# Fixing eight expert tiles in advance instead of four, over two experts, in a fused attention and mixture-of-experts kernel

## What is computed

```python
x = x + ((1-g)*layernorm(x) + g*(A + A.T)/2)   # per batch; A = sigmoid(sim) where sim is among
                                                # the 153 largest of its row, else 0
h = layernorm(x)                                # now 2048 tokens
logits = h @ router_weight.T + router_bias      # 16 experts
top_val, top_idx = top_k(logits, 4); score = softmax(top_val)
for each token and each of its 4 experts e:
    gate, up = split(h @ gate_up_proj[e] + gate_up_bias[e])      # 512 -> 2 x 512, interleaved
    gate = min(gate, 7); up = clip(up, -7, 7)
    y = ((up + 1) * gate * sigmoid(1.702*gate)) @ down_proj[e] + down_bias[e]
    out[token] += score * y
out = x + out
```

## Time and profile before

| | us |
|---|---|
| runs of the kernel before | 915.58 median, 914.37 to 919.76, 3 runs |
| the profiled execution | 910.78 |
| its span in the trace | 909.0 |

### The profile page before, as it was taken

How to read it: one execution, slowest core, us unless ns; L and a number is a source line. 1 busy time by engine, 2 the same in 40 slices (tenths; PEclk the granted TensorE clock), 3 DMA queues, 4 the chain that set the end, 5 groups by cost and what they waited for, 6 DMA issues and landing times.

```text
span 909.0 us, 16747 instructions
## 1 busy us (share of the span) xinstructions
PE 768.3 (85%) x3566; PEld 622.4 (68%) x3567; DVE 595.4 (65%) x1068; ACT 403.4 (44%) x663; POOL 311.6 (34%) x352
## 2 busy tenths in 40 slices
PE   5354825256699999999999999999999999999993
PEld 2123524245588888878888887887788878888882
DVE  3678948397484855875757667577757565766542
ACT  2999758622142523353333524435533253442221
POOL 1331736475323322232323333332323222332221
PEclk9765655556799999999999999999999999999998
DMA  8501102115564552655736465586557445632332
GB/s 279 196 1 47 47 12 82 48 48 159 151 162 122 140 136 55 179 165 141 210 64 191 111 187 133 136 217 185 144 163 187 95 101 164 177 94 47 57 58 42
DMA packets 70706, 112.06 MB, mean 123 GB/s; under 512 B 29894, under 2 KB 32198, under 8 KB 70598
## 3 DMA queue, kind: packets, MB, share of 16 engines
q1 hardware_dynamic: 32454, 74.22, 23.5%
q0 software_dynamic: 18416, 36.53, 20.3%
q10 hardware_dynamic: 19728, 0.15, 1.2%
HBM read 84.05 MB, written 28.90 MB: 124 GB/s over the span
## 4 chain that ended last, share of the span: by engine, by line
PE 72%; ACT 11%; DVE 5%; another core or an unknown queue 4%; issue 4%; POOL 2%; ACTq 1%; DMA 1%; DVEq 0%; SPq 0%; POOLq 0%
PE gate_up_ps L852 40%; PE bank L852 22%; PE bank L842 3%; PE bank L834 3%; ACT marks L518 3%; ACT bgu L518 3%; PE bank L736 1%; ACT x_sb L531 1%; POOL step_u L412 1%; ACT w L655 1%; ACT A L528 1%; ACT xn L549 1%; DMA gam<-n_L_xattn_gamma_raw_dram 1%; PE gate_up_ps L741 0%
## 5 line engine op out<-in xcount | busy, mean ns | idle before, releaser
L852 PE MATMUL gate_up_ps<-w,xh 128*128 (+1 forms) x1152 | 364.5, 398 | 1.5 <-DVE xl L1032 1.5
L852 PEld LDWEIGHTS gate_up_ps<-w,xh 128*128 128x128 f32 x1152 | 212.6, 190 | 42.8 <-issue 1.9
L437 POOL DMA_INDIRECT out_dram<-yb,aslot x72 | 131.9, 1832 | 286.8 <-ACT yb L636 254.0
L852 PE MATMUL gate_up_ps<-w,xl 128*128 (+1 forms) x576 | 226.2, 393 | 0.0
L852 PE MATMUL bank<-w,hh 128*128 (+1 forms) x576 | 179.5, 393 | 7.3 <-DVE hl L1037 6.2
L629 ACT ACTIVATE sg<-gc 128x512 f32<-128x512 f32 x72 | 45.6, 634 | 228.5 <-DVE gc L1047 211.7
L1043 DVE TENSOR_TENSOR gu<-gate_up_ps,bgu 128x1024 f32<-128x1024 f32 x72 | 88.1, 1224 | 76.5 <-PE gate_up_ps L852 47.4
L428 POOL DMA_INDIRECT xg<-xn_rows,gslot x75 | 76.1, 1015 | 179.1 <-DMA gslot<-slot_rows 149.3
L852 PEld LDWEIGHTS bank<-w,hh 128*128 128x128 f32 x576 | 107.1, 188 | 35.8 <-issue 14.1
L1037 DVE TENSOR_TENSOR hl<-bank,hh 128x512 fp32r<-128x512 f32 x72 | 49.5, 688 | 117.3 <-ACT hh L623 105.6
L852 PEld LDWEIGHTS gate_up_ps<-w,xl 128*128 128x128 f32 x576 | 108.9, 189 | 23.6
(11 more groups left out here) (209 smaller groups left out, 796.0 us busy)
## 6 DMA issues: line engine op xcount, KB each, us to landing
raw_w<-_L_ffn_gate_up_proj_dram SPq DMA_DIRECT2D x64, 512.0 KB
raw_w<-in_L_ffn_down_proj_dram SPq DMA_DIRECT2D x64, 256.0 KB
bgu<-n_gate_up_proj_bias_dram SPq DMA_DIRECT2D x16, 512.0 KB
x_sb<-in_x_dram SPq DMA_DIRECT2D x4, 1024.0 KB, 11.5
xn_rows<-xn SPq DMA_DIRECT2D x4, 1024.0 KB
out_dram<-x_sb SPq DMA_DIRECT2D x4, 1024.0 KB
xg<-xn_rows,gslot POOLq DMA_INDIRECT x75
out_dram<-yb,aslot POOLq DMA_INDIRECT x72
```

The source lines that it names most:

```text
L437: pool.indirect_dma_start(out_v, bass.IndirectOffsetOnAxis(aslot[:, k, 0:1], 0), yb[:, k % 2, :], None, bounds_check=TOKENS - 1, oob_is_er ...
L852: last = nc.tensor.matmul(out_ps, lhs[:, rows], w[:, bass.ds(buf, 1), part, c, cols].rearrange("p a d -> p (a d)"), start=(m == 0), stop=( ...
```

## The change

Eight tiles are fixed in advance: tiles 0 to 3 are the first four of expert 0, tiles 4 to 7 the first four of expert 1, all filled from batches 0 to 2. Behind them come the other tiles of expert 0, those of expert 1 (one at least), then experts 2 to 15 as before. The table of words so has 18 segments for 16 experts, with two small rows of corrections (`steps`, `rooms`) for where a segment's slots begin. Experts 0 and 1 hold the two buffers of `w` through the first four segments, so no weights move for the two extra changes of expert. `gslot` of tiles 4 to 7 is loaded by SP from fixed addresses between and behind expert 1's raw halves, and `gslot` of tiles 8 to 10 by the table. POOL gathers tile 4 before it waits for the write of x. Steps 4 to 7 are written without reads of the table on every engine. `split_first` stays in steps 2 and 3.

```diff
-FROZEN = UNROLL
+FROZEN = 2 * UNROLL
+SEGS = E + FROZEN // UNROLL
...
+        def first_block(T):
+            return T // UNROLL * (TOKENS // P) + T % UNROLL
...
             if known(T, FROZEN) and row == 0:
-                return 0
+                e, e_before = T // UNROLL, max(T - 1, 0) // UNROLL
+                return e | e << FIELDS["bias"][0] | e_before % 2 << FIELDS["buffer_before"][0]
...
                         sp.wait_ge(S["lo_done"], HALF * (h + 1))
                         load_half(1, h, 1)
+                        for T in range(UNROLL + 2 * h, UNROLL + 2 * h + 2):
+                            sp.wait_ge(gathered[T % UNROLL], 16)
+                            sp.dma_start(gslot[:, T % UNROLL, :], slot_d[first_block(T) * P:(first_block(T) + 1) * P, :]
+                                         ).then_inc(gslot_in[T % UNROLL], 16)
...
-            for T in range(1, UNROLL):
+            for T in range(FROZEN - 3, FROZEN):
                 k = (T + 3) % UNROLL
-                sp.wait_ge(gathered[k], 16)
+                sp.wait_ge(gathered[k], 32)
...
-            for T in range(FROZEN):
+            for T in range(UNROLL):
                 gather(T, T)
             scatter(NB, NT * TOP_K)
+            gather(UNROLL, 0)
+            pool.wait_ge(S["acc_out"], 16 * NB)
+            add(0, 0)
             pool.wait_ge(S["xn2_out"], 16 * NB)
-            pool.wait_ge(S["acc_out"], 16 * NB)
-            for T in range(1, FROZEN):
+            for T in range(2, FROZEN):
                 gather(T + 3, (T + 3) % UNROLL)
-                add(T - 1, T - 1)
+                add(T - 1, (T - 1) % UNROLL)
...
-                elif T >= FROZEN - 2:
-                    split_first(T - (FROZEN - 2))
+                elif T in (UNROLL - 2, UNROLL - 1):
+                    split_first(T - (UNROLL - 2))
...
-                    link(V.tensor_scalar(short[:], ps_cnt[:, 0:1], -1.0, float(FROZEN * P), ALU.mult, ALU.add))
+                    link(V.tensor_scalar(short[:], ps_cnt[:, 0:2], -1.0, float(UNROLL * P), ALU.mult, ALU.add))
...
-            link(V.tensor_scalar(til[:], til_i[:], 1.0, None, ALU.max))
+            send(V.tensor_scalar(til[:, 2:3], til_i[:, 0:1], 0.0, None, ALU.max))
+            send(V.tensor_scalar(til[:, 3:SEGS], til_i[:, 1:E], 1.0, None, ALU.max))
...
             def table_words():
-                link(V.tensor_tensor(held[:, 0:2, :], past[:, 0:2, :], turns[:], ALU.mult))
+                send(V.tensor_tensor(held[:, 0:2, :], past[:, 0:2, :], turns[:], ALU.mult))
+                link(V.tensor_tensor(held[:, 2, :], past[:, 1, :], steps[:], ALU.mult))
+                send(V.tensor_reduce(first_at[:], held[:, 2, :], AX.X, ALU.add))
```

More of the change, by code:

```diff
@@ L168, in xattn_moe_kernel @@
         fill = sb("fill", [P, E])
-        short = sb("short", [P, 1])
+        short = sb("short", [P, 2])
         token_id = sb("token_id", [P, NT], i32)
@@ L221, in xattn_moe_kernel @@
         near = sb("near", [P, 5])
-        turns = sb("turns", [P, 2, E])
+        turns, steps, rooms = sb("turns", [P, 2, SEGS]), sb("steps", [P, SEGS]), sb("rooms", [P, SEGS])
         til_i = sb("til_i", [P, E], i32)
-        til, cum, room = sb("til", [P, E]), sb("cum", [P, E]), sb("room", [P, E])
+        til, cum, room = sb("til", [P, SEGS]), sb("cum", [P, SEGS]), sb("room", [P, SEGS])
         spare = hotv[:].rearrange("p r k e -> p (r k e)")
-        past, held = (spare[:, i * 5 * E:(i + 1) * 5 * E].rearrange("p (t e) -> p t e", e=E) for i in range(2))
+        past, held = (spare[:, i * 5 * SEGS:(i + 1) * 5 * SEGS].rearrange("p (t e) -> p t e", e=SEGS) for i in range(2))
         which, block_at = sb("which", [P, 5]), sb("block_at", [P, 5])
-        move, flag = sb("move", [P, 4]), sb("flag", [P, 8])
+        move, flag, first_at = sb("move", [P, 4]), sb("flag", [P, 8]), sb("first_at", [P, 1])
         total_i = sb("total_i", [P, 1], i32)
@@ L317, in _ @@
                     sp.wait_ge(S["scat"], 16 * RT * TOP_K * EARLY)
-                    for k in range(FROZEN):
+                    for k in range(UNROLL):
                         sp.dma_start(gslot[:, k, :], slot_d[k * P:(k + 1) * P, :]).then_inc(gslot_in[k], 16)
@@ L688, in _ @@
             for T in range(FROZEN):
-                step(T, T)
+                step(T, T % UNROLL)
             act.wait_ge(S["table_done"], 1)
@@ L925, in join @@
                 dve.wait_ge(S["chain"], n[0])
-            dve.wait_ge(S["pool_c"], 13)
-            for at_bit, value, cells in ((17, 1.0, turns[:, 0, 0:E - 1:2]), (17, -1.0, turns[:, 0, 1:E - 1:2]),
-                                         (15, 1.0, turns[:, 1, 0:E - 1]), (15, -2.0, turns[:, 1, 2:E - 1:3])):
+            dve.wait_ge(S["pool_c"], 14)
+            last = SEGS - 1
+            for at_bit, value, cells in ((17, 1.0, turns[:, 0, 0:last:2]), (17, -1.0, turns[:, 0, 1:last:2]),
+                                         (15, 1.0, turns[:, 1, 0:last]), (15, -2.0, turns[:, 1, 4:last:3])):
                 link(V.memset(cells, value * (1 << at_bit)))
-            link(V.tensor_scalar(turns[:, 1, 0:E - 1], turns[:, 1, 0:E - 1], 1.0, None, ALU.add))
+            link(V.tensor_scalar(turns[:, 1, 0:last], turns[:, 1, 0:last], 1.0, None, ALU.add))
+            link(V.memset(turns[:, 1, 1:2], -1.0 * (1 << 15) - 1.0))
+            for cells, value in ((til[:, 0:2], UNROLL), (steps[:], TOKENS // P), (steps[:, 0:3], 0),
+                                 (steps[:, 0:1], -TILES), (steps[:, 2:3], TILES + TOKENS // P + UNROLL),
+                                 (steps[:, 3:4], TOKENS // P - UNROLL), (rooms[:], TOKENS // P),
+                                 (rooms[:, 1:2], UNROLL - TOKENS // P), (rooms[:, 3:4], TOKENS // P - UNROLL)):
+                link(V.memset(cells, float(value)))
             link(V.memset(pad_rows, 0))
@@ L1217, in _ @@
                 if b == EARLY - 1:
-                    send(V.tensor_tensor(slot0_e[:, 0:1], slot0_e[:, 0:1], short[:], ALU.add))
-                    link(V.tensor_tensor(fill[:, 0:1], fill[:, 0:1], short[:], ALU.add))
+                    send(V.tensor_tensor(slot0_e[:, 0:2], slot0_e[:, 0:2], short[:], ALU.add))
+                    link(V.tensor_tensor(fill[:, 0:2], fill[:, 0:2], short[:], ALU.add))
             dve.wait_ge(S["rank_ps"], NB)
@@ L1247, in table_words @@
                 last, last_1, last_2 = move[:, 1:2], move[:, 2:3], move[:, 3:4]
-                send(V.scalar_tensor_tensor(out=nth, in0=which[:, 1:2], scalar=-float(TOKENS // P), in1=block_at[:, 1:2],
-                                            op0=ALU.mult, op1=ALU.add))
+                send(V.tensor_tensor(nth, block_at[:, 1:2], first_at[:], ALU.subtract))
                 send(V.tensor_tensor(splits, last, last_1, ALU.max))
@@ L1261, in table_words @@
                 link(V.scalar_tensor_tensor(out=splits, in0=splits, scalar=4.0, in1=second, op0=ALU.mult, op1=ALU.add))
-                link(V.scalar_tensor_tensor(out=splits, in0=which[:, 1:2], scalar=float(E - 1), in1=splits,
+                link(V.scalar_tensor_tensor(out=splits, in0=which[:, 1:2], scalar=float(SEGS - 1), in1=splits,
                                             op0=ALU.is_lt, op1=ALU.mult))
@@ L1268, in _ @@
             table_words()
-            step(1, 1)
-            step(2, 2)
-            step(3, 3)
+            for T in range(1, FROZEN):
+                step(T, T % UNROLL)
             dve.wait_ge(S["table_in"], 32)
```

20 lines of the change are left out of this document (11 added, 9 removed).

## The result

| | us |
|---|---|
| the changed kernel | 935.72 median, 925.78 to 939.72, 4 runs |
| the kernel before, beside it | 915.62 median, 914.37 to 919.76, 4 runs |
| ratio | 1.0177, 95% interval 1.0115 to 1.0240 |
| the profiled execution, and its span | 937.34, 935.6 |

The account below looks back on a forecast made before the run. The prediction took PE's matmul stream, with 1% of slack, as the bound. It summed 5.8 + 1.95 - 0.5 + 0.9 = 8.1 us onto the 915.6 median, giving 923.7 us (+0.9%), with an 8-in-10 range of 915.5 to 929.

Parts of the forecast that it names:

- Steps 4 to 7 without table reads: Steps 4 to 7: the removed table reads stood ahead of PE's tile 4 with no idle time, so 0.
- the segment of three: Steps 10 to 13: expert 2's split moves from a segment of seven tiles into one of three, +0.9 us.
- a whole lap: Tile phase rival: padding pushes the total past 72 tiles and adds a lap, 36 us, 952; chance 0.02.
- What bounds the kernel: Tile phase: a PE stream of matmuls with 1% of slack; delays to it are added to the end.
- Cover for the table: Before tile 4: four fixed tiles already cover the table, so the gain from the change's aim is zero.
- Expert 1's weights two tiles earlier: Tile 4: PE's first half of gate_up(4) waits for split_first(1)'s last subtraction, a stop of 5.8 us.
- The clock after the stop: Behind the stop at tile 4: PE comes back at half rate, costing 1.95 us, bounds 0 and 4.7.
- the rival in which the clock stays up: After the stop at tile 4: no half rate, so 6.2 us in all, 921.8 us; chance 0.15.
- Taken over: After the stop at tile 4: DVE is free by the time hl(3) is due, a gain of 0.5 us.
- SP, POOL, DVE at 0: Added gslot loads, gather(4)'s earlier start, and DVE's memsets and small table instructions: all hidden, 0.
- not slower: Start: the 7.37 us wait on an unknown releaser vanishes, 916.3 us; 0.16 together with a hidden stop.
- Slower by over 1%: Whole kernel above 924.7 us, chance 0.38; its upper-bounds rival at tile 4 and the three-tile segment: 926.9, 0.22.

Follow-up runs that it names:

- e1: The changed kernel run again unaltered, for a second trace: 933.82 us, ratio 1.0239.
- e2: The changed kernel with 16 semaphore increments put on ACT before its first wait: 923.4 us, ratio 1.0108.
- e5: The changed kernel with split_first a step earlier (steps 1 and 2), without padding: 921.92 us, ratio 1.0111.
- e7: The changed kernel with 96 semaphore increments ahead of ACT's first wait: 924.03 us, ratio 1.0138.
- e9: e2 with the stop at tile 4 filled by doing gate_up(4)'s first half twice with expert 0's weights: 890.47 us, ratio 1.0040.
- e3: e2 with split_first a step earlier, in steps 1 and 2: 914.88 us, ratio 1.0014.
- e10: The changed kernel with 56 semaphore increments ahead of ACT's first wait: 893.72 us, ratio 1.0088.
- e8: The kernel before, with expert 1's raw weights loaded only after DVE has read tile 0's first products: 910.92 us, ratio 1.0000.
- after: The changed kernel in its first measurement and profile: 935.72 us, ratio 1.0177.
- e4: The kernel before with 112 semaphore increments ahead of ACT's first wait: 924.61 us, ratio 1.0142.
- e6: The changed kernel with 16 semaphore increments behind ACT's loop of laps: 931.58 us, ratio 1.0232.

## Why the prediction was wrong, and where it was right

**The step that failed** is "Steps 4 to 7 without table reads ... 0". I priced the removed reads by the idle time ahead of tile 4, and there they are worth nothing, as said. What I did not price is that instructions taken out ahead of a loop move the loop, and that the loop's cost depends on where it stands. It measured 10.5 us between the profiled executions (9.57 to 14.56 and 9.09 to 14.55), 10.4 us between the medians of e1 and e2, and 10.0 in e5. No rival had it either: they lay at tile 4, at the start, in the segment of three, or in a whole lap. With e2's 16 increments, which put this right and nothing else, the kernel measures 8.8 us above before (923.4 - 914.56) where the sum was 8.1.

**What bounds the kernel.** Right, and it is why ACT's stall is paid: PE has 1% of slack. `hh` came 4.5 us later behind the branch than in e2 (6.72 against 2.21) and the period grew by 5; in e7 3.1 and 2.8 us of ACT became 1.7 and 2.1 of the period. But "nothing behind makes it good" was also a reason to look behind tile 59, where the code changes from written-out tiles to a loop, and the prediction never spoke of that part.

**Cover for the table.** Right as far as the runs go: none was faster than the kernel before.

**Expert 1's weights two tiles earlier, 5.8 us.** The stop was 5.6 us, put down to `split_first`'s line as said. e9 measures it without the clock: 15.27 - 9.06 = 6.2 us. And "nothing lets the split begin earlier" was true of the code as it stood, but e3 shows how little it took: a step earlier, and the raw half is there in time.

**The clock after the stop, 1.95 us.** The mechanism is shown by e9. The size was 5.38 - 2.73 = 2.65 us in the profiled execution, 5.35 in e2 and 4.63 in e10, so 1.9 to 2.7. The transposes behind came at 0.44 instead of the 0.9 I had written: the stretch at half rate (1.2 GHz) fell wholly on the half of gate_up. The rule of the Trainium skill on oscillation ("TensorE: Matmul & The Clock Gate", "HAM oscillation — how this bites in real kernels") holds here for a stop of 5.6 us too; the rival in which the clock stays up fell for the kernel as it is.

**Taken over, -0.5.** Measured -0.4 (T = 5: 9.59 to 9.19). **The segment of three, +0.9.** Measured +0.8 (T = 12 up by 1.19, T = 10 down by 0.35), and T = 12 is 10.2 in every run with the eight fixed tiles. From step 10 to 13 the changed kernel takes 28.4 us, where 28.3 was forecast. **SP, POOL, DVE at 0**: nothing in the periods contradicts it, no run tried them alone.

**The start.** The rival "not slower" hung on the wait on an unknown releaser. It was 7.37 us before, 7.8 in the changed kernel and 6.7 in the next execution of the same program, 12.1 in e2, 4.7 to 6.6 in e5 to e8, and is absent on the third chip. No run shows it to be the change's, and what it is stays open. tr_h(0), which follows it, moved by 6.0 us in one execution of the changed kernel and by 0.6 in the next, so a difference between two single executions can hold that much.

**The chances.** "Slower by over 1%" had 0.38, for reasons that gave 926.9, or 952 with a lap more; the outcome that came true needed a mechanism that I had not listed. The lap more (952) did not come: 72 adds.

**A better version.** None beats the kernel before. With the loop moved and the split a step earlier (e3) the eight fixed tiles are level with it, which fits a cover for the table that was long enough with four tiles.

## What to carry to other kernels

When an edit changes how many instructions an engine has ahead of a loop that runs at the end's pace, count the packets of the instruction queue inside the loop's stretch, before and after: here none went with no stop, some per turn meant a stall of 2 to 7 us a turn, and a few dead instructions ahead of the loop can take it away. Compare kernels step by step rather than by totals: here the periods named three separate costs of 8, 1 and 10 us where the totals held 6 us of chance as well. And a stop of 5.6 us in a stream of matmuls cost its length and then 1.9 to 2.7 us of half rate; filling it with matmuls that nobody needs saved most of the second part.

## What the runs showed of the hardware

**Code of a loop is read again or not, by its place.** A shift of 16 instructions took 10 us off two turns; with one of 96 about 4 of them stayed. The Trainium skill ("Runtime: NRT & Kernel Launch", "Instruction fetch mechanics") says that an engine's memory for instructions is small, is filled in order, and that a taken branch out of the present window makes the engine wait for a fetch. The trace agrees: 2.73 us from the branch of the loop on (some 0.2 us where the code is not read again), and 1.48 us more within the turn. It also says that crossing from one block to the next is mostly hidden: that fits the written-out tiles, where the queue reads code all the time and most periods are 9.05 to 9.09, and not the 1.48 us, which come inside the turn and behind no branch back. It gives blocks of 16 KiB; here the queue that reads at the turns has 81 packets of 8 KB (not ACT's alone, perhaps), and packets of 16 KB (0.54 MB in 33) are on the other instruction queue. That the packet is what the place is counted in was my guess; six places fit it, and a block of twice the size too. How much of the body of 313 instructions must fit, and into what, stays open.

**The price of a turn isn't fixed.** It is 4.8 to 7.0 us at T = 65 and 69 in after, e1, e4, e5 and e6, with two stops per turn, and 2 us in e7 with one stop, though it reads about as many packets.

**Chips differ ahead of the tiles.** The kernel before measured 914.56, 911.91 and 886.77 us on three. It was not traced on the third, but e2 and e10, which differ by the padding, were traced on the first and the third: of 32.8 us between them 31.5 lie ahead of tr_h(0).
